# The experts' down product from high and low parts, the low weights fetched per tile

## The reference

```
h      = rmsnorm(layernorm(x)) * norm_w                 # 256 values
logits = h @ gate_w.T + gate_b                          # 8 experts, the best two are kept
t1     = h @ mlp1_w[e].T + mlp1_b[e]                    # 512 values: glu and lin, interleaved
act    = min(glu,7) * sigmoid(1.702*min(glu,7)) * (clip(lin,-7,7) + 1)   # 256 values
y      = act @ mlp2_w[e].T + mlp2_b[e]                  # the "down" product, 256 values
out    = x + softmax-weighted sum of the two chosen y
```

## Time and profile before

| what | value |
|---|---|
| median of 3 runs | 2119.84 us (2117.81 to 2120.19) |
| the profiled execution's own time | 2112.28 us |
| its span | 2110.3 us |
| PE busy | 2014.0 us, 95% |
| DVE, ACT, POOL busy | 74%, 68%, 54% |
| granted TensorE clock, mean | 0.988 of full speed |
| experts 0 and 1, as windows | 905 to 1130 us, 1865 to 2110 us |

### The profile page before, as it was taken

The page is one execution under the profiler, slowest core; times in us unless marked ns, Lnnn a source line. Parts: engine busy times, 40 slices in busy tenths (PEclk is TensorE's granted clock), DMA queues, the critical chain, the costliest instruction groups (busy, mean ns, idle before and its releaser), DMA issues.

```text
span 2110.3 us, 39468 instructions
## 1 busy us (share of the span) xinstructions
PE 2014.0 (95%) x11622; PEld 1615.6 (77%) x11622; DVE 1557.6 (74%) x4611; ACT 1436.2 (68%) x3757; POOL 1139.0 (54%) x1342
## 2 busy tenths in 40 slices
PE   7899999999999999899998999999999999989995
PEld 6677777878777777678886787878878787778884
DVE  7877768686868685858776867776776777757777
ACT  5777868686868686745554877777777767655445
POOL 4765556465555554444434566666667565534432
PEclk8999999999999999999999999999999999999998
DMA  4334512121212110424451342131322212244448
GB/s 139 140 137 149 159 33 84 44 79 48 79 48 69 59 43 17 167 79 130 135 168 64 125 147 93 65 109 45 119 74 84 74 65 71 103 153 127 146 135 280
DMA packets 79527, 215.55 MB, mean 102 GB/s; under 512 B 12884, under 2 KB 47988, under 8 KB 76760
## 3 DMA queue, kind: packets, MB, share of 16 engines
q1 hardware_dynamic: 66360, 176.58, 25.9%
q0 software_dynamic: 12960, 36.46, 5.0%
HBM read 155.51 MB, written 128.81 MB: 135 GB/s over the span
## 4 chain that ended last, share of the span: by engine, by line
PE 77%; DVE 11%; ACT 6%; issue 3%; DMA 2%; POOL 1%; SPq 0%; DVEq 0%; ACTq 0%; POOLq 0%
PE bank L630 6%; PE bank L650 5%; PE bank L612 5%; PE bank L2313 5%; PE bank L1541 5%; PE bank L597 3%; PE bank L2267 3%; PE bank L2269 3%; PE bank L598 3%; PE bank L2268 3%; PE bank L1526 3%; PE bank L1442 2%; PE bank L1444 2%; PE bank L1443 2%; PE bank L543 2%
## 5 line engine op out<-in xcount | busy, mean ns | idle before, releaser
L1164 POOL TENSOR_TENSOR P<-P,rc 128x128 f32<-128x128 f32 (+3 forms) x512 | 359.1, 732 | 348.6 <-DVE rc L962 348.4
L954 DVE CUSTOM_DVE_ANT_0 P<-bank,tab 128x512 f32<-128x512 f32 (+3 forms) x512 | 244.3, 491 | 108.8 <-PE bank L598 105.1
L777 ACT ACTIVATE P<-P,mn 128x128 f32<-128x128 f32 (+3 forms) x512 | 281.7, 552 | 36.7 <-DVE mn L954 33.0
L2598 POOL DMA_INDIRECT yD<-Yf,place x142 | 140.4, 989 | 249.5 <-ACT Yf L2378 237.5
L788 ACT COPY PT<-bank 128x512 f32<-128x512 f32 (+1 forms) x384 | 194.1, 516 | 101.3 <-PE bank L612 94.3
L2036 POOL TENSOR_TENSOR rf<-rp 128x512 f32<-128x512 f32 x128 | 165.6, 1294 | 138.0 <-DVE rp L1868 136.4
L2047 POOL TENSOR_TENSOR q<-rf,q 128x512 fp32r<-128x512 f32 x128 | 163.3, 1298 | 121.2 <-ACT q L1662 120.9
L612 PE MATMUL bank<-cst,P 128*128 128x128 f32 x1280 | 207.0, 276 | 14.9 <-POOL P L1164 8.9
L597 PE MATMUL bank<-q 128*128 128x512 f32 (+3 forms) x512 | 185.4, 373 | 16.9 <-DVE mn L954 13.5
L612 PEld LDWEIGHTS bank<-cst,P 128*128 128x128 f32 x1280 | 152.7, 141 | 43.0 <-POOL P L1164 12.7
L930 DVE TENSOR_TENSOR q<-bank,q 64x512 fp32r<-64x512 f32 x256 | 175.8, 687 | 7.2 <-ACT q L768 1.3
(11 more groups left out here) (267 smaller groups left out, 5884.8 us busy)
## 6 DMA issues: line engine op xcount, KB each, us to landing
hS<-in_c_fill SPq DMA_DIRECT2D x128, 544.0 KB, 4.0
Gf<-hS SPq DMA_DIRECT2D x142, 136.0 KB
yg<-yD SPq DMA_DIRECT2D x14, 512.0 KB, 4.7
W1lf<-w1lD SPq DMA_DIRECT2D x12, 512.0 KB, 7.3
X<-in_x SPq DMA_DIRECT2D x8, 512.0 KB, 5.5
stage<-in_w SPq DMA_DIRECT2D x8, 512.0 KB, 3.7
w1hD<-W1A SPq DMA_DIRECT2D x8, 512.0 KB
w1lD<-stage SPq DMA_DIRECT2D x8, 512.0 KB
```

What stands on the lines that cost most here:

```text
L777: i = e.activation(ps, ps, ACT.Exp, bias=mn[:, pb, t:t + 1], scale=-1.0, accum_out=rs[:, pb, t:t + 1])
L954: e.tensor_tensor_reduce(out=P[:, pb, OFF[t]:OFF[t] + w], in0=score(h, t), in1=tab[:, 512 - w:512], scale=-SLOPES[h % 16], scalar=3e38, op ...
L1164: i = e.tensor_tensor(ps, ps, rc[:, h % 3, t:t + 1].broadcast_to([128, w]), ALU.mult)
```

## The change

The down product is made of three float32r matmuls per half of K. Its high weights are kept in `W2` as before (now in float32r and read from `w2hD`), its low weights do not stay in SBUF: each tile fetches the 256 KB of its expert from `w2lD` into a ring of three places. `ATh` is what ACT copied into `AT`; the low part `ATl` is a new DVE instruction (`turned_low`). The last multiply of the activation goes to POOL, but for 12 of the 71 tiles (`ON_VECTOR`), and writes over `li`. Splitting `w2` is done by POOL in attention A, one expert (128x512) after the scales of each unit with p > 5 in batches 1 to 4, with transfers of 256 KB by SP around it.

```diff
-ROWS_AT = (18, 19, 20, 21, 25, 26, 27, 28)
+ROWS_AT = (18, 20, 21, 23, 25, 27, 28, 30)
+ON_VECTOR = [0, 1, 2, 6] + [a + 3 for a in ROWS_AT]
...
 # attention A, scalar: gate_high
+                        if kc == 0 and 0 < bt < 5:
+                            e.wait_ge(d_w1o, 32 * E + 48 + 64 * bt)
 # attention A, gpsimd
+                    def split_w2(i):
+                        raw, H = stage[:, 0], stage[:, 1].bitcast(F32R)
+                        e.wait_ge(d_w1s, 32 * E + 16 * i + 16)
+                        e.tensor_copy(H, raw).then_inc(p_w1, 1)
+                        e.wait_ge(p_w1, 2 * (E + i) + 1)
+                        e.tensor_tensor(raw.bitcast(F32R), raw, H.bitcast(F32), ALU.subtract).then_inc(p_w1, 1)
...
+                        if 0 < bt < 5 and p > 5:
+                            split_w2(2 * bt + p - 8)
 # attention A, sync
+                    def fetch_w2(i):
+                        e.wait_ge(d_w1o, 32 * E + 48 + 32 * i)
+                        e.wait_ge(q.m_lg, 2 * (i // 2) + 2)
+                        e.dma_start(stage[:, 0], T["w2"][:, i].rearrange("p k n -> p (k n)")).then_inc(d_w1s, 16)
+                    def store_w2(i):
+                        e.wait_ge(p_w1, 2 * (E + i) + 1)
+                        e.dma_start(w2hD[:, i], stage[:, 1]).then_inc(d_w1o, 16)
+                        e.wait_ge(p_w1, 2 * (E + i) + 2)
+                        e.dma_start(w2lD[:, i], stage[:, 0]).then_inc(d_w1o, 16)
...
 # experts, tensor
                     def flip_a(a):
-                        e.wait_ge(v_ac, T0 + a + 1)
+                        e.wait_ge(*activated(a))
                         if a:
-                            e.wait_ge(a_at, T0 + a)
+                            e.wait_ge(v_at, low_turned(a - 1))
...
                     def down(a):
-                        e.wait_ge(a_at, T0 + a + 1)
+                        e.wait_ge(v_at, low_turned(a))
+                        e.wait_ge(d_wl[a % 3], landed(a))
...
                         for kc in range(2):
-                            i = e.matmul(o, AT[:, k, kc], W2[:, ex, kc]..., start=False, stop=kc == 1)
+                            wh = W2[:, ex, kc].rearrange("p x n -> p (x n)")
+                            e.matmul(o, ATh[:, k, kc], wh, start=False, stop=False)
+                            e.matmul(o, ATh[:, k, kc], low_weights(a)[:, kc], start=False, stop=False)
+                            i = e.matmul(o, ATl[:, k, kc], wh, start=False, stop=kc == 1)
 # experts, vector: act() now also waits for f_a of tile a-3
                     def act_end(a):
+                        if a in ON_VECTOR: (as before, into ac = li)
+                    def turned_low(a):
+                        src = bank[3][:, 0:256].rearrange("p (a b) -> p a b", a=2)
+                        e.wait_ge(a_at, T0 + a + 1)
+                        e.tensor_tensor(ATl[:, a % 2], src, ATh[:, a % 2].bitcast(F32), ALU.subtract).then_inc(v_at, 1)
...
                             act(a + 3)
+                        if a + 1 < NS:
+                            turned_low(a + 1)
 # experts, gpsimd
                             scatter(a - 1)
+                        if a + 3 < NS:
+                            act_end(a + 3)          # if a + 3 is not in ON_VECTOR
 # experts, sync
+                    def load_low(a):
+                        if a in (0, L1):
+                            e.wait_ge(r_et, 2 * ph + (2 if a else 1))
+                        if a > 2:
+                            e.wait_ge(f_dn, T0 + a - 2)
+                        ex = e.value_load(etab[0:1, a:a + 1], min_val=0, max_val=E - 1)
+                        low = w2lD[:, bass.ds(ex, 1)].rearrange("p x n -> p (x n)")
+                        e.dma_start(low_weights(a)...., low).then_inc(d_wl[a % 3], 16)
+                    if last:
+                        e.wait_ge(q.m_o, NU)
+                    for a in range(3):
+                        load_low(a)
                     for a in range(4, NS):
                         load(e, ph, q, a)
+                        if a > 7:
+                            load_low(a - 5)
...
+                    for a in range(NS - 5, NS):
+                        load_low(a)
+                        if last and a in (NS - 5, NS - 3, NS - 1):
+                            store_out(...), fetch_rows(...)      # one batch each, as before the loop's end
```

More of the change, by code:

```diff
@@ L469, in attention_a @@
                 q.spare = nc.sbuf_base + 2 * TT * D * 4
+                q.late = R2 + 78496
                 X = b("X", [128, 3, TT, D])
@@ L1267, in sync @@
                         if bt and bt + 1 < NB:
-                            fill_paced(e, 0, q, bt, bt + 1, range(5, 8))
+                            fills(bt, range(5, 8))
                         if bt == 0:
@@ L2198, in experts @@
                     Wh, Wl = WhB, WlB
+                    with ExitStack() as early:
+                        reach(R2 + 57 * 1024, "gap_r", early)
+                        rings = [sb("ring0", [128, 3, 2, D], F32R, early)]
                     reach(R2 + 60 * 1024, "gap_8", c)
@@ L2224, in x_bank, with low_weights, landed, low_turned @@
                     return bank[3 if a == 1 else (2, 5)[a % 2]]
+                def low_weights(a):
+                    return rings[a >= RING_MOVES][:, a % 3]
+                d_wl, v_at, p_ac = q.d_x, q.v_xT, q.n_p
+                def landed(a):
+                    return 16 * len(range(a % 3, NB, 3)) + 16 * (a // 3 + 1)
+                def low_turned(a):
+                    return 2 * NB + a + 1
+                def activated(a):
+                    if a in ON_VECTOR:
+                        return v_ac, ph * len(ON_VECTOR) + ON_VECTOR.index(a) + 1
+                    return p_ac, (2, 1)[ph] * NU + a + 1 - sum(n <= a for n in ON_VECTOR)
                 chosen_expert = {}
@@ L2559, in vector @@
                     act_end(2)
+                    turned_low(0)
                     for a in range(NS):
@@ L2599, in scatter, with act_end @@
                                              None).then_inc(d_y[a % 4], 16)
+                    def act_end(a):
+                        if a not in ON_VECTOR:
+                            e.wait_ge(v_gl, 3 * (T0 + a) + 3)
+                            e.wait_ge(a_sg, T0 + a + 1)
+                            e.tensor_tensor(ac[:, a % 3], li[:, a % 3], sg[:, a % 3], ALU.mult).then_inc(p_ac, 1)
                     scores_over(e)
```

71 lines of the change are left out of this document (45 added, 26 removed).

## The result

| | kernel before | changed kernel |
|---|---|---|
| median | 2119.51 us (6 runs, 2117.81 to 2121.97) | 2130.53 us (6 runs, 2122.86 to 2137.71) |
| profiled execution, span | 2112.28, 2110.3 us | 2122.86, 2121.0 us |

The ratio is 1.0049, 95% interval 1.0035 to 1.0063: the change makes the kernel 0.5% slower, some 10 us. The forecast was 2112.6 with 64% on faster. The range, 2103 to 2127, does not hold the time.

A forecast was written before the change was run, and what follows sets the result against it. The prediction took PE's instruction order to bound the expert tiles. Terms: -16.0 + 3.6 + 4.2 + 1.0 = -7.2 us, so the profiled 2112.28 becomes 2105.1 and the median, 7.6 above, 2112.6; range 2103 to 2127.

The forecast's parts named there:

- POOL in attention A: Splits delay POOL's scaling 0.2 us in each of four units, 1.0 us taken; their transfers, stores and SP waits cost nothing.
- PE's part: Down product of each expert tile: 0.87 us removed, six matmuls of 0.72 us added, tile falls from 2.80 to 2.65.
- the small terms of either sign in the full stretches: Expert iterations where DVE is as full as PE: small gains and losses taken together as nothing.
- The gain of 16.0: Experts: 0.15 us for each of 54 tiles of experts 0 and 52 of experts 1, 16.0 us gained.
- The wait for `turned_low`: Before each tile's down product PE waits for DVE's new instruction; 0.9 us are spare, so no cost was taken.
- rival B: In the experts PE waits for DVE, tiles stay near 2.80 us: 2117 to 2125, middle 2120; chance 0.16.
- Experts 0 around a = 64: Low weights of tiles 60 and 61 land 1.2 and 2.4 us late behind other transfers: 3.6 us lost.
- Experts 1, the end: Low weights of tiles 60 to 70 add 8.8 us of transfers, 7.7 us are free: middle taken, 4.2 us lost.
- The prediction's own signs of being wrong: In the experts: plain tile not 2.65 us, or the two transfer stretches costing under 3 us together or over 13.
- Rival C: In expert tiles POOL's multiply and a DVE instruction, both reading two SBUF tiles, exclude each other: 2140; 0.14 with other losses.

The follow-up runs named there:

- k2: The kernel before plus only the change's splits of the down weights in attention A, experts unchanged: ratio 1.0045 to the kernel before.
- m1: k2 with its eight splits one batch later, nothing else of the change: ratio 0.9998 to the kernel before.
- k4: The changed kernel unaltered, run a third time beside the kernel before on one chip: ratio 1.0049.
- f2: The changed kernel with splits one batch later and low weights fetched only for the first three tiles of each place of the ring: ratio 0.9978 to the kernel before.
- h2: f3 with every tile's multiply on DVE and none on POOL: ratio 1.0003 to the kernel before.
- f1: The changed kernel unaltered, run again beside its variants on one chip: ratio 1.0053 to the kernel before.
- h3: f3 with the five remaining low fetches at the end of experts 1 asked for before SP's wait to store the second finished batch: ratio 1.0000 to the kernel before.
- f3: The changed kernel with splits one batch later and attention B's first transfers spread over more tiles of experts 0: ratio 0.9989 to the kernel before.
- k1: The kernel before, run as a variant of itself: ratio 0.9998.
- e1: The changed kernel with all eight splits of the down weights one batch later in attention A: ratio 1.0010 to the kernel before.
- e4: The changed kernel with the eight `put_rows` in every second iteration, 18 to 32, their DVE multiplies moving along: ratio 1.0069 to the kernel before.
- h1: f3 with the multiplies of the eight tiles behind `put_rows` moved to POOL as well: ratio 0.9981 to the kernel before.
- h4: f3 with the edits of both h1 and h3: ratio 0.9982 to the kernel before.
- k3: f2 with the multiplies of the eight tiles behind `put_rows` moved to POOL: ratio 0.9960 to the kernel before.
- m2: h1 run a second time, on the other kind of chip: ratio 1.0005 to the kernel before.

## Why the prediction was wrong

**The step that failed** is the last of "POOL in attention A": "Transfers of these splits, their stores and the waits of `gate_high` and SP have whole units of time: nothing; SP's fills behind them are needed a batch later." I asked who waits for the fills behind a fetch, and not what stands in front of it. The fills of batch 0 and 1 still filled SP in batch 1; POOL, in order, waited with the scaling of the attention behind it, and PE with it. This costs 9.5 us (k2: 1.0045, and by its interval 6.4 to 12.7), or nothing one batch later (m1), where the prediction had 1.0. In k2's trace the heads fall 8.2 us back at this place, 5.9 us of it PE's wait, the rest from 6.83 us at half clock; 2.5 come back before the experts by a chance that the last section tells of, so the trace of attention A shows some 6 us net, and what makes up the rest of the 9.5 stays open. Its other half, that a split makes the scaling at p = 6 late by 0.2 us each time, isn't seen: in the first trace of the change the heads behind unit 15 keep their distance to within 0.1 us, in k2 and k4 to within 0.4 over all later splits together.

**PE's part**: right. A plain tile is 2.66 us; over 33 plain iterations 4.5 to 4.8 us are gained where 33 x 0.14 makes 4.6, and the six matmuls are 0.12 apart.

**"I ... take the small terms of either sign in the full stretches as nothing together"**: mis-sized. DVE's work in 18 to 24 came out as the prediction worked it out, 20.17 against 20.3 us, but the lag isn't carried. By f2, where no transfer can be the cause, iterations 1 to 5 lose 0.78 and 0.14 us, 19 to 25 1.27 and 0.93, and the stretches from 63 on 2.00 and 1.72, together 6.8 us where nothing stood. The gain of 16.0 also counted tiles 67 to 70, which lie in a full stretch, and 0.15 us a tile where 0.14 came; f2's other stretches sum to -13.2. Part of the 6.8 is POOL's multiply beside DVE: with all multiplies on DVE, iterations 63 to 69 of experts 0 cost 0.07 less than in the kernel before instead of 2.0 more (h2), while 1 to 5 get worse.

**The wait for `turned_low`**: no cost in plain tiles, as forecast; rival B fell with the tile at 2.66.

**Experts 0 around a = 64**: predicted 3.6. Measured, with the 0.57 that four plain tiles would have gained, 5.5 to 6.1 us; 1.2 of it are there without the fetches too (f2), so they cost 4.9. Place and cause are right (no low fetches: 0.63; transfers spread: 1.22). Missing was the half clock behind the wait. The low weights of tile 60 also took longer from their issue than worked out, 7.7 us (1102.50 to 1110.15) against 5.8; that the eight transfers issued behind them share the engines with them would explain it and was not tested alone.

**Experts 1, the end**: predicted 4.2. From 59 on f1 is 1.9 us above f2 (0.77 + 4.71 - 2.94 against -0.44 + 1.72 - 0.63), so the low transfers cost about 2 us, and the lost part is paid back: PE's last tiles are late, but the end hangs on DVE's sums and the stores (h3).

**The sum with measured terms**, from the ledger: f2's experts are -6.3 (-13.2 in the plain stretches and the last tiles, +6.8 in the full ones), f1's +1.2, so the low transfers cost 7.6, 4.9 of it around tile 60 and 1.9 at the end. With attention A that is -6.3 + 7.6 + 9.5 = +10.8, against +10 to +12 measured. The experts for themselves are a draw: 1.0049 with them, 1.0045 without. Hence the answer to "where did 16 us go": 6.8 to a full DVE, 7.6 to the low transfers, the rest to tiles that were counted as plain and were not, and the sign is set by one fetch in attention A. The prediction's own signs of being wrong would not have told: the plain tile is 2.66, and the two transfer stretches cost 6.8 us together, between its 3 and 13. They watched the terms that it had priced, and not the one that it had put at nothing. And the 7.6 us that it found between the median and the profiled execution of the kernel before are the two kinds of chip. f3 (0.9989) has the split and the transfers mended, and the highest bound of its interval is just under 1; no variant with the full work beat the kernel before on both kinds of chip.

**Rival C** named a mechanism that exists, and its price was wrong: a plain tile did not grow. POOL's multiply starts when DVE's L2535 has ended, because it needs its result, so the two-input instruction of the plain tile never meets it. What it meets is `turned_low` (112 times in f1, mean 0.417 us, 0.416 without it). But the pieces of attention B's low weights do meet it (L2552, above: 4.5 us of DVE's time), and so do DVE's last sums, which also have two inputs in SBUF. L2605 has a median of 1.23 us. DVE's timeline of f1, then POOL's:

```profile
2080.80 1.66 DVE L2605 TENSOR_TENSOR xrf<-xrf,roomf 128x1024 f32<-128x1024 f32 x1
```

```profile
2080.64 0.74 POOL L2682 TENSOR_TENSOR lif<-lif,sgf 128x256 f32<-128x256 f32 x1 [0.64 <-DVE lif L2535]
```

The Trainium skill (SBUF — State Buffer, Who interferes with whom) calls this an exclusive lock of a port pair that DVE and GpSimd share. The traces agree on who is slowed: the instruction with one PSUM input is not, those with two SBUF inputs are. Here L2605 took 0.43 us more than its median where the multiply had 0.58 left to run when it started, somewhat less than a full lock for that time would make.

## What to carry to other kernels

A fetch put into a queue is as late as what stands in front of it on that engine: read the issuing engine's timeline ahead of the new place as closely as the engine that waits. Where an engine was full before, a lag is not carried but paid; count such stretches at their full surplus. And before a stall in one trace is explained, look for it in a second execution, and in one of the kernel before on the same chip: the best-looking stalls of the first trace here belong to the kind of chip, and the kernel before has them there too.

## What the runs showed of the hardware

**Half clock by chance.** PE's granted clock falls to 0.50 (1.2 GHz) for 3.41 us, at some places 6.83, after some short idle stretches and not after others. In f1 and in f2 PE is idle for some 0.85 and 0.53 us at the same two points of a unit of attention B, and L1520 to L1522 follow; the windows that begin 0.7 us behind the first L1520, f1 first (us, PE busy, PEclk, DMA share, GB/s):

```profile
1680.70:1684.10 3.40, 3.40 (x10) 0.50 0.00 0
```

```profile
1667.60:1671.00 3.40, 3.40 (x17) 1.00 0.01 2
```

Ten matmuls of 128x512 against 17. One such stretch makes all that follows about 1.5 us late; between 40 us and the end's last 50, f1 has 41 us of them and f3 has 17. The mean granted clock of f1's runs is 0.9840 against 0.9885 for the kernel before: here the change, which adds waits, paid for them again in clock.

**A held DVE in the kernel before.** An instruction of 8 columns took 3.44 us, from 845.16 until POOL's scaling ended at 848.58 (DVE, then POOL):

```profile
845.16 3.44 DVE L388 TENSOR_SCALAR dd<-f 128x8 f32<-128x8 f32 x1
```

```profile
845.83 2.75 POOL L1164 TENSOR_TENSOR P<-P,rc 128x128 f32<-128x128 f32 x4
```

It is there again in k1, and also in e1, e4, f3 and h3; in the other fourteen traces the same instruction took 0.17 us, and in the changed kernel, k2 and m1 the heads behind it are 2.5 us nearer to before's than the heads ahead of it. So these 2.5 us come and go, with the change and without it. The two cases differ by a few hundredths of a microsecond: in the six traces the instruction starts 0.32 to 0.33 us behind the start of POOL's second indirect transfer (844.84 in the trace of before), in the fourteen 0.28 to 0.30. Why that decides is not shown.

**Stalls of all engines but PE, on one kind of chip.** In the first trace of the change ACT waited 3.8 to 4.3 us, at iteration 28 of experts 0 and at 21 and 28 of experts 1, for matmuls that had long ended; SP's instructions there were 0.7 us apart. The second kind of chip shows it for the kernel before too (k1, iterations 20 and 27; the profile calls the releaser of such a wait "remote"; ACT's waits from 985 to 1030):

```profile
ACT ATf L2372 <- remote: 6.6, 2, 4.0
```

On that kind of chip the stalls lie where `put_rows` are neighbours: at iterations 19 to 21 and 27 in k1 and k2 (`put_rows` at 18 to 21 and 25 to 28), at 21 and 28 in the change's two traces (at 20 and 21, 27 and 28), and they are absent from the three traces in which the multiplies of these tiles are on POOL (h1, h4, k3). So they need DVE's multiply in these tiles; whether they need the neighbours too, a spread `ROWS_AT` on that kind of chip would tell, and was not run.

The traces of that kind of chip hold fewer semaphore records, 19,197 for the changed kernel where f1, the same program, has 23,427. That the recording of the profile holds up the engines there fits both, and was not tested. The Trainium skill says (NOTIFIC — the notification-queue block, section 7.1) that this block's internal pipeline always holds back its producers rather than lose a record; no run here can show it, and it does not say why records would be missing. The difference between the two kinds of chip is some 7 us (5.8 of it in k1's stretches of the ledger), and it is what h1, h4 and k3 gained on the second kind: in their traces these stalls are absent, and m2, on the first kind of chip, has no gain.
